# One added wait: the loads of destination rows behind the gathers of the same pair

## The reference, cut to what matters

```
h = relu(layernorm(x))
Wh = h @ W + b
Wr, Wc = Wh[src], Wh[dst]                       # one row of each for every edge
sim = sum(Wr * Wc) / max(|Wr| * |Wc|, 1e-8)
base = edge_weight * softplus(...) * (src != dst)
prop_pos = segment_sum(base * relu(sim) * Wc, src)
prop_neg = segment_sum(base * -relu(-sim) * Wc, src)
x = x + scale * (c0 * prop_pos + c1 * prop_neg + c2 * Wh)
```

## Time and profile before

| | us |
|---|---|
| median of 3 runs | 5184.12 |
| lowest, highest run | 5181.92, 5193.49 |
| span of the profiled execution | 6621.9 |
| setup | 0 to 92 |
| first edge stage | 92 to 2080 |
| second layer's edge stage | 2080 to 3180 |
| third layer's | 3180 to 4560 |
| fourth layer's first | 4560 to 5840 |
| the rest | 5840 to 6621 |

### The profile page before, as it was taken

How to read it: one execution, slowest core, us unless ns; L and a number is a source line. 1 busy time by engine, 2 the same in 40 slices (tenths; PEclk the granted TensorE clock), 3 DMA queues, 4 the chain that set the end, 5 groups by cost and what they waited for, 6 DMA issues and landing times. The chain is left out here.

```text
span 6621.9 us, 101200 instructions
## 1 busy us (share of the span) xinstructions
PE 4686.8 (71%) x28712; PEld 3011.7 (45%) x28712; DVE 4162.0 (63%) x7696; ACT 1910.3 (29%) x6351; POOL 3158.1 (48%) x2950
## 2 busy tenths in 40 slices
PE   4777777777777666666566666664777777739999
PEld 2333333333334333333445444453444444418998
DVE  4445445444446666666566666664676766688998
ACT  2333333333333000000233333331000000016775
POOL 5333333433332655555344544442566666615554
PEclk6878788887878888888587888776998888969998
DMA  3222222222221111111111111111343334411111
GB/s 98 54 52 52 51 54 55 54 53 52 53 51 32 40 42 36 42 39 34 26 39 41 40 38 41 40 38 35 107 110 107 111 108 119 112 52 49 49 49 36
DMA packets 493009, 379.51 MB, mean 57 GB/s; under 512 B 345991, under 2 KB 379152, under 8 KB 492888
## 3 DMA queue, kind: packets, MB, share of 16 engines
q1 hardware_dynamic: 395352, 288.65, 15.4%
q0 software_dynamic: 90560, 83.37, 7.0%
q10 hardware_dynamic: 6976, 6.23, 0.3%
HBM read 341.76 MB, written 36.12 MB: 57 GB/s over the span
## 5 line engine op out<-in xcount | busy, mean ns | idle before, releaser
L1066 POOL DMA_INDIRECT edge_src_rows<-table_wh,edge_gather_idx x806 | 784.6, 973 | 1213.6 <-DVE edge_small L1185 928.0
L1095 PE MATMUL edge_sums_ps<-edge_onehot_src,edge_halves 128*128 128x512 bf16 x4840 | 1045.0, 360 | 298.3 <-issue 289.3
L933 POOL DMA_INDIRECT edge3a_src_rows<-table_h,edge3a_gather_idx x808 | 762.6, 944 | 558.0 <-issue 313.4
L2096 PE MATMUL edge3a_z_ps<-Wz,edge3a_both_ends_t 128*128 128x396 f32 x1616 | 698.2, 582 | 357.2 <-DVE edge3a_terms L2189 318.0
L1171 DVE TENSOR_SCALAR edge_onehot_src<-layer_node_row,edge_src_col,edge_magnitude 128x1568 bf16<-128x1568 f16 x605 | 412.5, 683 | 845.8 <-remote 583.4
L933 POOL DMA_INDIRECT table_cat<-table_hn,table_gather_idx x592 | 598.1, 1010 | 636.1 <-PE edge_cat_t_ps L1776 344.4
L1457 POOL DMA_INDIRECT edge_src_rows<-table_h,edge_gather_idx x608 | 607.6, 999 | 532.9 <-issue 182.1
L1095 PEld LDWEIGHTS edge_sums_ps<-edge_onehot_src,edge_halves 128*128 128x128 f16 x4840 | 427.6, 104 | 864.3 <-issue 525.0
L2189 DVE SCALAR_TENSOR_TENSOR edge3a_terms<-edge3a_z_ps,att_z 128x792 f32<-128x792 f32 x404 | 385.6, 977 | 401.4 <-DMA edge_edge_attr<-in_ea 219.0
L2096 PEld LDWEIGHTS edge3a_z_ps<-Wz,edge3a_both_ends_t 128*128 128x128 f32 x1616 | 334.0, 217 | 660.5 <-DVE edge3a_terms L2189 364.6
L2508 PE MATMUL edge3b_sums_ps<-edge3b_onehot,edge3b_weighted 128*128 128x128 f32 x4848 | 572.3, 278 | 6.4 <-DVE layers_accT L2546 4.6
(11 more groups left out here) (366 smaller groups left out, 8334.3 us busy)
## 6 DMA issues: line engine op xcount, KB each, us to landing
edge_dst_row<-in_dst_row SPq DMA_DIRECT2D x102, 512.0 KB
edge3a_dst_row<-in_dst_row SPq DMA_DIRECT2D x102, 512.0 KB
edge_window<-table_wh SPq DMA_DIRECT2D x816, 32.5 KB
edge3a_window<-table_h SPq DMA_DIRECT2D x816, 32.0 KB
edge_edge_attr<-in_ea SPq DMA_DIRECT2D x101, 256.0 KB
kept_rows<-edge3a_src_rows SPq DMA_DIRECT2D x101, 256.0 KB
edge3b_src_rows<-kept_rows SPq DMA_DIRECT2D x101, 256.0 KB
edge_edge_attr<-in_ea SPq DMA_DIRECT2D x101, 128.0 KB
```

The costliest lines, as they stand in the source:

```text
L933: nc.gpsimd.indirect_dma_start(self.slot(b, j), None, self.table[:, :], bass.IndirectOffsetOnAxis(ap=self.idx[b][:, j:j + 1], axis=0)).the ...
L1066: nc.gpsimd.indirect_dma_start(g[q][:, j, :], None, k.t_wh[:, :], bass.IndirectOffsetOnAxis(ap=idx[q][:, j:j + 1], axis=0)).then_inc(gathe ...
L1095: mm = pe.matmul(acc[:, i, 0:w], halves[q][:, j, a, :, :].rearrange("p h d -> p (h d)"), hot[:, o:o + w], start=first and a == 0, stop=False)
L2096: mm = pe.matmul(zp[q % 2][:, i, 0:H * ZH], hcT[h][:, j * P:(j + 1) * P], k.Wz[:, :], start=True, stop=True)
```

## The change

SP waits, ahead of the window loads of pair t, until all gathers of pair t have landed as well. Nothing else is altered: the same transfers, in the same order on each engine.

```
--- before.py
+++ after.py
@@ -1048,6 +1048,7 @@
                         sp.dma_start(drow[h][:, :], k.dst_row[bass.ds(2 * t + h, 1), :].to_broadcast([P, ROWS])
                                      ).then_inc(rows_loaded[h], 16)
                     wait_past(sp, wc_ready, 3 * t - 3)
+                    sp.wait_ge(gathered[q], 16 * (PB * m + tiles_of(t)))
                     for h in (0, 1):
                         for j, base in enumerate(window_starts(nc, k, SP, t, h)):
                             sp.dma_start(win[q][:, h * B + j, :], k.t_wh[bass.ds(base, P), :]
```

## The result

The changed kernel takes 5872.41 us (median), the kernel before 5185.1 beside it: ratio 1.1322, 95% interval 1.1306 to 1.1337. One of its four runs took 9004.79 us; the median is of all four, the ratio and its interval are made from the other three (5866.04, 5869.05, 5875.77). It is slower by 687 us; 568 were forecast, and the range of 5340 to 5900 held it. Its own recorded execution has a span of 5864.2 us and is one of the timed runs (5866.04). That is the first surprise: a recorded execution is as long as a timed one here. The forecast had put the 1438 us between 6621.9 and 5184 down to recording.

A forecast was written before the change was run, and what follows sets the result against it. Unrecorded, the first edge stage was taken as PE-bound at 26.5 us a pair; the wait makes a 38.1 us loop the bound. 49 x (38.1 - 26.5) = +568 us gives 5752 us, range 5340 to 5900.

The forecast's parts named there:

- the 1438 us: Profiled span 6621.9 us against the 5184 us median of timed runs; the excess was read as event recording holding up sequencers.
- The loop: First edge stage: gathers, landing, window loads, next index load, next gathers, nothing overlapping; 38.1 us a pair, the new bound.
- Its terms: Loop parts: gathers 22.5, landing 2.5, window registers 1.0, windows to index load 9.6, index load to gather 2.5 us.
- PE's pace before: Time of an unrecorded, PE-bound pair in the first edge stage: 26.5 us taken, between 25.2 and 27.8.
- the good stretch: First edge stage time when PE's matmuls follow without pauses: 145 matmuls in 25.2 us, granted clock 0.92.
- The 38.6 us and the 13.4 us of the bad stretch: First edge stage: a profiled pair takes 38.6 us, 25.2 good plus 13.4 with PE's matmuls held at issue.
- the two arguments for it: For an unstalled pace: SP register moves stretching to 1387 ns; later stages' busy PE, 3134 us, exceeding the 3104 left.
- The sum against the profile's own time: Change measured against the profiled pace of the first edge stage: 49 x (38.1 - 38.6) = -25 us.
- Rival 1: Gathers and window loads hinder each other in every run; separating them gains 118 us, giving 5066; chance 0.08.
- Rival 2: Gathers quicker unrecorded, without 0.30 us between them: loop 29.7 us, +157 us, giving 5341; chance 0.11.
- Rival 3: Wait hidden if indices are early enough: windows 35.6 us after norms, PE's work 34.6; about 5184; chance 0.04.
- Rival 4: PE's clock stays at its lower level, 1.2 GHz: a pair takes 50.4 us, +1171, giving 6355; chance 0.04.

The follow-up runs named there:

- opening it (5444): Changed kernel with the index load of pair t+1 moved ahead of the wait, only windows held back: 5444.06 beside 5185.97 for the kernel before, ratio 1.0498.
- shortening it (5637): Changed kernel with the wait between the first eight and last eight window loads of a pair: 5636.71, ratio 1.0865 to the kernel before.
- closing a smaller one (5379): No wait ahead of the windows; the index load of pair t waits for the gathers of pair t-1: 5378.59, ratio 1.0364 to the kernel before.
- the run that stands for it: Changed kernel with the wait in the same place but for the gathers of pair t-1: 5197.13, ratio 1.0023 to the kernel before.

## Why the prediction was right, and where it was wrong

- **The loop.** Right, and for the reason given. It was priced at 38.1 us and is 38.6 in the middle of the stage. That it is a loop, closed by the index load behind the wait, is shown by opening it (5444) and by shortening it (5637); closing a smaller one (5379) goes the same way.
- **Its terms.** The nearness of the sum is in part luck. From the eighth pair to the forty-eighth the sixteen starts of the gathers take 23.4 us on average (22.5 priced), while the way from the last gather to the first window, from there to the index load and on to the gather take 3.3 + 9.3 + 2.55 = 15.1 (15.6 priced). The two errors take each other back by half.
- **PE's pace before.** The term that was mis-sized. I took 26.5 us, halfway between 25.2 and 27.8; where it could be measured it is 25.2, the lower end, which is the sum over the good stretch of the earlier trace rows. The upper end took the 15 matmuls that the good stretch lacks for lost speed; 25.2 says that only their records were missing.
- **The start.** Left out of the sum without a reason: the wait also holds the first windows, and PE begins 22.6 us later (83.9 for 61.3). With what was measured it is 49 x (38.6 - 25.2) + 23 = 680 us in place of 568: 64 more from PE's pace, 25 from the loop, 23 from the start. Another 11 us, of 687, lie between the kernel before and the run that stands for it.
- **The 38.6 us and the 13.4 us of the bad stretch.** (1980.0 - 48.1) / 50 is a mean over the stage with its quick start. In the middle of the same trace (335.6 to 1860.8, 39 loads) a pair takes 40.1 us:

```profile
L1045 SPq DMA_DIRECT2D edge_gather_idx<-in_src_t x39: 2/333/333, 335.6 to 1860.8; - x39
```

- **The 1438 us.** The step that failed: "I read as the recording of events". No run shows a recorded execution that is longer than its own time. A trace of before from the second kind of chip has the same length and the same long register moves as the one that the forecast was read from, and the 5184 us are met on the first kind alone; that the two came from different chips is inferred from this. The pace of the good stretch was the right one for 5184, yet the two arguments for it are of unequal worth. The register move of 1387 ns holds: none longer than 38 ns is in a trace from a chip where the kernel before takes 5184. The totals came out right by luck. PE's busy time behind the stage isn't the same on both kinds of chip (3195 and 2935 us in the two rows above), so the 3134 of the trace say little of the 5184. And "a span that hardly moves or falls" came true (6621.9 to 5864.2) only because the second trace was taken on another kind of chip.
- **The sum against the profile's own time**, -25 us: met on a chip of the kind that the trace came from, -28, with luck. It compares 38.1 with 38.6 where 38.66 stands against 39.95, and leaves out the later start.
- **Rival 1** (the recorded pace is the true one) is true on that kind of chip, in kind if not in size: faster by 0.4%, not by 118 us. By its own condition it loses where a pair takes less than the loop, and that is the chips of the 5184.
- **Rival 2** (quicker gathers) is refuted: the median gather takes 0.94 to 0.95 us, with 0.30 between two, on both kinds of chip; among them are executions that were themselves timed at 5201 and 5866 us.
- **Rival 3** (hidden) isn't met even with the index load ahead: a second path of some 60 us over two pairs holds PE, +258 us. I had counted it from the norms to the windows and left out the way back to the norms.
- **Rival 4** (clock) happens for 7 us a pair, and hides in the slack of the loop: PE isn't in the ring, and has caught up when the next windows land.
- **The rules of the Trainium skill.** The Trainium skill's "DMA: Bandwidth & Descriptors" (Rules for kernel authors) says to issue early and wait late; these runs agree with it (1.1322). In the trace a gather is long beside a tensor_tensor: the cast ends at 1017.29 and the gather that starts at 1017.71 takes 2.72 us, to 1020.43; a tensor_tensor covers 1017.32 to 1019.61, and a one-hot the time up to 1020.21:

```profile
1016.06 1.23 DVE L1260 CAST edge_halves<-edge_weighted 128x2048 f16<-128x2048 f32 x1
1017.32 2.29 DVE L1264 TENSOR_TENSOR edge_halves<-edge_weighted,edge_halves 128x2048 f16<-128x2048 f32 x1
1019.53 0.68 DVE L1172 TENSOR_SCALAR edge_onehot_src<-layer_node_row,edge_src_col,edge_magnitude 128x1568 bf16<-128x1568 f16 x1
```

Undisturbed that gather would have ended at 1018.65, in the middle of the tensor_tensor, before the one-hot began. That is not what the inference alone would give, and it is in line with the reading of the indices being held up. No run separates these, nor the tensor_tensor from the one-hot, so this stays an observation.

What stays open: why some chips stretch the instructions of SP and PE when gathers and window loads run together, why only 7 us after the first window load, and why the stages that follow take some 800 us more there. Recording may have a part in it, since no execution here went without it for certain; no run tells. Nor was the stage timed by leaving it out on a chip of the first kind, and the changed kernel with its index load ahead, whose windows run beside the next pair's gathers, never came to one of the second.

## What to carry to other kernels

A wait on an issuing queue costs what is queued behind it, and not only what it guards: here 428 of 687 us came from one load behind it. Follow the queue to the next iteration: if something there feeds the very thing waited for, the wait has closed a loop, and the loop's length, added up from the trace, is the new period. Read a period in the middle of a stage; a mean over all of it contains the start. And when a trace's span and the timed runs differ by a quarter, first ask whether they come from the same chip; a sum should be made for both paces, as the sign of a change can hang on it.

## What the runs showed of the hardware that was not expected

- Two kinds of chips: the same kernel takes 5184 to 5186 us on one and 6615 to 6693 on the other, stable within each job. On the second, register moves of SP take up to 1423 ns while gathers and window loads run together, and PE's matmuls start about 0.7 us or a multiple of it apart (2.13 and 1.43 here, in the kernel before). Once the wait keeps gathers and window loads apart, no register move exceeds 38 ns in this stage on the same chip.

```profile
1007.98 0.38 PE L1095 MATMUL edge_sums_ps<-edge_onehot_src_act,edge_halves 128*128 128x512 bf16 x1 [1.05 <-issue]
1010.11 0.59 PE L1095 MATMUL edge_sums_ps<-edge_onehot_src_act,edge_halves 128*128 128x512 bf16 x1 [1.76 <-issue]
1011.54 0.19 PE L1095 MATMUL edge_sums_ps<-edge_onehot_src_act,edge_halves 128*128 128x32 bf16 x1 [0.84 <-issue]
```

- After 9.5 us without work PE is granted 0.57 of its clock for 7 us (a tile takes 2.66 us, the lower of the two levels), then 1.00.
